# Two ConvLSTM recurrences: seven packed 128-row operands in place of nine 112-row ones, and whole-row elementwise operations

## The reference, cut to what matters

```python
def _convlstm_scan(x_rows, w_mid, b, reverse):
    # x_rows: (H, B, C, W); w_mid: (4*HC, C+HC, 3)
    def step(carry, xr):
        h, c = carry
        inp = jnp.concatenate([xr, h], axis=1)
        gates = lax.conv_general_dilated(inp, w_mid, (1,), 'SAME', dimension_numbers=dn) + b[None, :, None]
        i, f, g, o = jnp.split(gates, 4, axis=1)
        c2 = jax.nn.sigmoid(f) * c + jax.nn.sigmoid(i) * jnp.tanh(g)
        h2 = jax.nn.sigmoid(o) * jnp.tanh(c2)
        return ((h2, c2), h2)
    _, hs = lax.scan(step, (z, z), x_rows, reverse=reverse)
    return hs
```

## Time and profile before

| | |
|---|---|
| Time, median of 3 runs (lowest to highest) | 2120.07 us (2117.99 to 2121.75) |
| The profiled execution: time, span of its instructions | 2124.06 us, 2122.2 us |
| PE matmul busy | 1832.6 us (86%) |
| DVE busy | 1387.2 us (65%) |
| ACT busy | 1066.5 us (50%) |
| POOL busy | 765.1 us (36%) |
| Mean granted TensorE clock | 0.936 |
| DMA | 111.26 MB, 20.7% of the 16 engines' span |

### The profile page before, as it was taken

How to read it: one execution, slowest core, us unless ns; L and a number is a source line. 1 busy time by engine, 2 the same in 40 slices (tenths; PEclk the granted TensorE clock), 3 DMA queues, 4 the chain that set the end, 5 groups by cost and what they waited for, 6 DMA issues and landing times. The chain is left out here.

```text
span 2122.2 us, 43782 instructions
## 1 busy us (share of the span) xinstructions
PE 1832.6 (86%) x16306; PEld 1197.3 (56%) x16306; DVE 1387.2 (65%) x2552; ACT 1066.5 (50%) x1961; POOL 765.1 (36%) x581
## 2 busy tenths in 40 slices
PE   6979179999999998459999999998503999999999
PEld 5535157777777775137777777776101455555555
DVE  5539968888888886658888888888541333333334
ACT  1116147777777775737777777776611222222220
POOL 2010055666666653036666566564029000000000
PEclk9989689999999999769999999999756999999999
DMA  2769420000000000930000000000760011101100
GB/s 74 250 193 201 105 54 22 22 24 22 22 24 22 22 24 13 168 97 23 24 22 23 23 22 24 22 22 9 125 170 0 3 32 32 33 18 33 32 18 25
DMA packets 74138, 111.26 MB, mean 52 GB/s; under 512 B 11248, under 2 KB 30560, under 8 KB 74032
## 3 DMA queue, kind: packets, MB, share of 16 engines
q1 hardware_dynamic: 74032, 109.65, 20.7%
HBM read 71.87 MB, written 37.75 MB: 52 GB/s over the span
## 5 line engine op out<-in xcount | busy, mean ns | idle before, releaser
L668 PE MATMUL gates_l<-xh_l,w_hi_l 112*112 112x512 f32 x3072 | 819.7, 402 | 106.3 <-DVE keep_l L730 106.3
L668 PEld LDWEIGHTS gates_l<-xh_l,w_hi_l 112*112 112x112 f32 x3072 | 537.9, 175 | 304.8 <-issue 107.2
L644 POOL TENSOR_TENSOR xh_l<-xf_l,xh_l 48x512 fp32r<-48x512 f32 x256 | 359.9, 1406 | 281.8 <-ACT xh_l L687 281.3
L668 PE MATMUL gates_l<-xh_l,w_lo_l 112*112 112x512 f32 x1536 | 450.4, 402 | 0.0
L639 POOL TENSOR_TENSOR xh_l<-hs,xh_l 48x512 fp32r<-48x512 f32 x254 | 303.6, 1195 | 173.7 <-DVE hs L759 173.7
L668 PEld LDWEIGHTS gates_l<-xh_l,w_lo_l 112*112 112x112 f32 x1536 | 270.0, 176 | 98.0
L1132 PE MATMUL b_dw<-b_hid,b_diag 32*32 32x512 f32 x9120 | 312.4, 599 | 0.0
L699 ACT ACTIVATE gate_if_l<-gates_l 112x512 f32<-112x512 f32 x256 | 153.4, 599 | 246.0 <-PE gates_l L668 246.0
L739 DVE TENSOR_TENSOR keep_l<-gate_if_l,cell_l 48x512 f32<-48x512 f32 x256 | 175.5, 686 | 140.7 <-ACT gate_if_l L699 140.7
L1132 PEld LDWEIGHTS b_dw<-b_hid,b_diag 32*32 32x32 f32 x9120 | 186.4, 103 | 114.4 <-issue 46.9
L748 DVE TENSOR_TENSOR cell_l<-keep_l,add_l 48x256 f32<-48x256 f32 x512 | 196.8, 428 | 26.6
(11 more groups left out here) (148 smaller groups left out, 1288.3 us busy)
## 6 DMA issues: line engine op xcount, KB each, us to landing
xf_l<-rows SPq DMA_DIRECT2D x256, 96.0 KB, 2.0
hs<-rows SPq DMA_DIRECT2D x32, 384.0 KB, 10.6
rows<-hs SPq DMA_DIRECT2D x32, 384.0 KB, 5.1
xr<-in_x_rows SPq DMA_DIRECT2D x24, 256.0 KB, 2.7
xc<-in_x_cols SPq DMA_DIRECT2D x24, 256.0 KB, 3.0
mixed<-stage SPq DMA_DIRECT2D x24, 256.0 KB, 3.0
edged<-stage SPq DMA_DIRECT2D x24, 256.0 KB, 3.2
mixed_sb<-mixed SPq DMA_DIRECT2D x32, 192.0 KB, 7.3
```

Of the source, the lines that this page charges most:

```text
L644: pool.tensor_tensor(xh[far[d]:far[d] + C, d, s, 1, :, 1:W + 1], xf[far[d]:far[d] + C, s, :].rearrange("p (b w) -> p b w", b=B), xh[far[d] ...
L668: mm = nc.tensor.matmul(ps[d][m][0:K, :], weight[:, d, m, t, :], xh[0:K, d, s, part, :, t:t + W], start=(first and t == 0), stop=(last and ...
```

## The change

The nine operands of 112 rows become seven of 128 rows. The 16 rows beside each 48 (48 to 63 and 112 to 127), which were padding, now hold 32 of the 48 x channels in their high part. The other 16 channels of x, with their three taps laid side by side on the partitions, once for the high and once for the low part of the weights, and the bias, make one operand of their own (xc). So the operands are: xc once; three taps of the tile HI (high part of h, low part of x, 32 channels of the high part of x); three taps of the tile LO (low part of h, a copy of the high part of h, the same 32 channels). With two halves m of the gates there are 14 matmuls in a half-step.

To fill these rows, ACT rounds both directions' x of a row in one operation of 112 rows into a new tile xs (split_hi, L746), copies the high part of the state to the far partitions (copy_state, L752), and SP copies the 16-row pieces within SBUF by four DMAs for each half-step (spread, L628 and L633). The low part of x (split_lo) now waits until the matmuls of two rows before have read the tile.

The elementwise work loses its halves: one tanh of the cell over 512 columns, one product for h_hi. tanh(g) is written in place in PSUM, i*g too, and the cell and its tanh take one bank of PSUM each for both directions. Before the loop, the weights (1568 KB in place of 588 KB) are loaded into the unused part of hs, rounded with two casts and turned into low parts by four masked operations. ACT begins its first split_hi only when DVE has set the first values of the semaphores behind these.

The diff, cut to its core:

```diff
+                def spread(d, s):
+
+                    for a in range(2):
+                        some = x_rows(s, slice(far[d] + a * GAP, far[d] + (a + 1) * GAP)).bitcast(F32)
+                        sp.dma_start(xh[a * HALF + C:(a + 1) * HALF, d, s, :, :].bitcast(F32), some.unsqueeze(1).broadcast_to([GAP, 2, FLAT])
+                                     ).then_inc(x_spread[d][s], 16)
+                    rest = xs[far[d] + 2 * GAP:far[d] + C, s, LEAD - 1:LEAD - 1 + FLAT].bitcast(F32)
+                    shifts = bass.AP(rest.tensor, rest.offset, [list(rest.ap[0]), [1, 3], [1, FLAT]])
+                    for c in range(2):
+                        sp.dma_start(xc[3 * GAP * c:3 * GAP * (c + 1), d, s, :].bitcast(F32), shifts).then_inc(x_spread[d][s], 16)
...
+                    sp.wait_ge(x_hi, s + 1)
+                    for d in range(2):
+                        spread(d, s)
+                sp.wait_ge(x_lo[0], 1)
+                sp.wait_ge(x_lo[1], 1)
+                load(2, H - 3, 0)
...
+                        done, ahead, split = (held(sp, 2 * k + (s + n)) for n in (1, 2, 3))
+                        row_f, row_b = split, held(sp, k * -2 + (H - 4 - s))
+                        if s < more:
+
+                            sp.wait_ge(x_lo[0], ahead)
+                            sp.wait_ge(x_lo[1], ahead)
+                            load(row_f, row_b, 1 - s)
+                        for d in range(2):
+                            sp.wait_ge(gates[d][1], done)
+                            if d == 0:
+                                sp.wait_ge(x_hi, split)
+                            spread(d, s)
...
+                            pe.wait_ge(x_spread[d][s], SPREAD * k + SPREAD)
+                            pe.wait_ge(sig_if[d], 2 * k + (s + 1))
+                            pe.wait_ge(sig_o[d], 2 * k + (s + 1))
+                            pe.wait_ge(cells[d], 2 * k + (s + 1))
+                            for m in range(2):
+                                chunk(m, 0, xc[:, d, s, :], 1, first=True)
+                            pe.wait_ge(x_lo[d], 2 * k + (s + 1))
+                            pe.wait_ge(h_hi[d], 2 * k + (s + 1))
...
+                                    chunk(m, 1 + t, xh[:, d, s, HI, :], t)
+                            pe.wait_ge(h_copy[d], 2 * k + (s + 1))
+                            pe.wait_ge(h_lo[d], 2 * k + (s + 1))
...
+                                for t in range(3):
+                                    mm = chunk(m, 4 + t, xh[:, d, s, LO, :], t, last=(t == 2))
+                                mm.then_inc(gates[d][m], 1)
...
+                    act.wait_ge(h_hi[d], 1)
+                    act.wait_ge(cells[d], 1)
+
+                def split_hi(t, r):
+
+                    act.wait_ge(x_in[r], 16 * t - 16 * r + 32)
+                    if not (isinstance(t, int) and t < 2):
+
+                        for d in range(2):
+                            act.wait_ge(x_spread[d][r], (t - r) * (SPREAD // 2))
+                            act.wait_ge(x_lo[d], t - 1)
+                    nc.scalar.activation(inner(x_rows(r, slice(0, K))), wide(xf[0:K, r, :]), ACT.Copy).then_inc(x_hi, 1)
+
+                def copy_state(t, d, s):
+
+                    n, f = near[d], far[d]
+                    act.wait_ge(h_hi[d], t + 1)
+                    nc.scalar.activation(inner(xh[f:f + C, d, s, LO, :]), inner(xh[n:n + C, d, s, HI, :]).bitcast(F32),
+                                         ACT.Copy).then_inc(h_copy[d], 1)
+                for r in range(3):
+                    split_hi(r, r % 2)
+                copy_state(0, 0, 0)
...
+                            if d == 0:
+                                copy_state(2 * k + s, 1, s)
+                            elif not (last and s == 1):
+                                copy_state(2 * k + (s + 1), 0, 1 - s)
+                            act.wait_ge(cells[d], 2 * k + (s + 2))
+                            nc.scalar.activation(tanh_c[f:f + C, :], cell[f:f + C, :], ACT.Tanh).then_inc(tanhs[d], 1)
+                        if s < more:
+                            split_hi(2 * k + (s + 3), 1 - s)
...
+                dve.wait_ge(w_loaded, 32)
+                per_d = NCH * 2 * K
+                for d in range(2):
+                    nc.vector.tensor_copy(w[:, d].rearrange("p a b c -> p (a b c)"), raw[:, d * per_d:(d + 1) * per_d]
+                                          ).then_inc(w_hi, 1)
+                for d in range(2):
+                    dve.wait_ge(w_hi, d + 1)
+                    for q, chunks in enumerate((slice(0, 1), slice(1, 4))):
+                        part = w[:, d, chunks].rearrange("p a b c -> p (a b c)")
+                        whole = raw[:, d * per_d + chunks.start * 2 * K:d * per_d + chunks.stop * 2 * K]
+                        nc.vector.scalar_tensor_tensor(part, part.bitcast(F32), mask[:, d, q:q + 1], whole, ALU.mult, ALU.add
+                                                       ).then_inc(w_ready, 1)
+                dve.wait_ge(cleared, 3)
+                for d in range(2):
+                    for i, first in enumerate((h_hi[d], h_lo[d], sig_if[d], sig_o[d])):
+                        nc.vector.memset(begun[:, 4 * d + i:4 * d + i + 1], 0.0).then_inc(first, 1)
...
+                            nc.vector.tensor_tensor(ps[d][1][n:n + C, :], gate_if[n:n + C, d, :], ps[d][1][n:n + C, :],
...
+                            nc.vector.tensor_tensor(cell[f:f + C, :], keep[n:n + C, :], ps[d][1][n:n + C, :], ALU.add
+                                                    ).then_inc(cells[d], 1)
+                            dve.wait_ge(sig_o[d], 2 * k + (s + 2))
+                            dve.wait_ge(tanhs[d], 2 * k + (s + 1))
+                            nc.vector.tensor_tensor(inner(xh[n:n + C, d, 1 - s, HI, :]), wide(gate_o[f:f + C, d, :]),
+                                                    wide(tanh_c[f:f + C, :]), ALU.mult).then_inc(h_hi[d], 1)
```

More of the change, by code:

```diff
@@ L539, in lstm_scans @@
     K = HALF + C
-    PART = HB * W
-    parts = [slice(j * PART, (j + 1) * PART) for j in range(2)]
+    GAP = HALF - C
+    FLAT = B * WP
+    LEAD = 2
     with ctx:
@@ L650, in _, with step @@
                         split_lo(s, d, s)
-                step(0)
-                with pool.Fori(1, H // 2 - 1) as k:
+                def step(k, last=False):
+                    for s in range(2):
+                        for d in range(2):
+                            if not last:
+                                split_lo(2 * k + (s + 2), d, s)
+                            if not last or s == 0:
+                                state_lo(2 * k + s, 2 * k + s if d == 0 else k * -2 + (H - 1 - s), d, s)
+                with pool.Fori(0, H // 2 - 1) as k:
                     step(k)
@@ L661, in _, with chunk @@
                         for d in range(2):
-                            pe.wait_ge(x_lo[d], 2 * k + s + 1)
-                            pe.wait_ge(h_hi[d], 2 * k + s + 1)
-                            def taps(m, weight, part, first, last):
+                            def chunk(m, q, tile, lo, first=False, last=False):
+                                return nc.tensor.matmul(ps[d][m][0:K, :], w[:, d, q, m, :], padded(tile)[:, :, lo:lo + W],
+                                                        start=first, stop=last)
@@ L667, in taps @@
+                            for m in range(2):
                                 for t in range(3):
-                                    mm = nc.tensor.matmul(ps[d][m][0:K, :], weight[:, d, m, t, :],
-                                                          xh[0:K, d, s, part, :, t:t + W],
-                                                          start=(first and t == 0), stop=(last and t == 2))
-                                return mm
+                                    chunk(m, 1 + t, xh[:, d, s, HI, :], t)
@@ L703, in step @@
-                            if not last:
-                                split_hi(k + 1, d, s)
-                            for j, part in enumerate(parts):
-                                act.wait_ge(cells[d], 4 * k + 2 * s + (j + 3))
-                                nc.scalar.activation(tanh_c[f:f + C, j, 0:PART], cell[f:f + C, j, 0:PART],
-                                                     ACT.Tanh).then_inc(tanhs[d], 1)
-                with act.Fori(0, H // 2 - 1) as k:
-                    step(k)
```

235 lines of the change are left out of this document (113 added, 122 removed).

## The result

| | before | after |
|---|---|---|
| Time, median of 5 runs (lowest to highest) | 2121.35 us (2117.99 to 2124.64) | 2137.75 us (2136.33 to 2145.22) |
| Ratio, after to before (95% interval) | | 1.0086 (1.0064 to 1.0108) |
| Profiled execution: time, span | 2124.06, 2122.2 | 2141.19, 2139.4 |
| First DMA of the first layer to its first sigmoid | 16.7 us | 32.1 us |
| Mean half-step | 4.293 us | 4.231 us |

The changed kernel is slower by 0.9%: 16.4 us by the medians, 17.2 us by the spans. Of the 17.2, the two starts add 15.4 and 15.3, together 30.7, the 254 half-step intervals give back 254 x 0.062 = 15.8, and the two tails add 2.4. What is left is -0.1. Three of the 23 executions of the kernel before that experiments 1 to 4 are compared with took 2211 to 2221 us, a slower state that occurs now and then, and the ratios leave them out.

The account below looks back on a forecast made before the run. DVE's cycle through the tanh was taken to bound the half-step at 4.24 us, saving 14 us, with later starts adding 28: 2124.06 - 14 + 28 = 2138, less 4.0 for the median, 2134 us; range 2100 to 2172.

Parts of the forecast that it names:

- DVE's cycle: From one h_hi to the next, through all DVE operations of a half-step and one tanh: 4.24 us against 4.295.
- The upper bounds: DVE's cycle with every term at its upper bound, given as 4.35 us.
- PE's 3.34: 14 matmuls at 0.239 us per half-step; rival that PE stays the bound, 1906 us, chance 0.02.
- the lower ones: DVE's cycle with every term at its lower bound, given as 4.03 us.
- hs to keep, held: On DVE, the other direction's keep is held until hs ends: 0.68 and 0.03, a step of 0.71 us.
- The rival cycle of 4.14: On DVE, hs and the next keep overlap, giving 4.14 us; part of the shorter-cycle rival, chance 0.22.
- tanh to h_hi, 0.10 because of two waits: Hand-over from ACT's tanh to L823 takes 0.10 us, not 0.03, since L823 has two waits.
- from add to cell: On DVE, 0.10 us from the end of add to cell, which needs add's result.
- The start: Each layer's first DMA to its first sigmoid takes 31 us; 14 us later per layer, 28 in all.
- SP: Ten DMA issues a row take 4.5 us of 8.48; rival that SP or DMAs bound, 2210 us, chance 0.04.
- Who releases PE before LO: Sign in the profile: PE idle before a half-step's first LO matmul, put down to POOL's h_lo.
- The tail: The end of each layer stays as it was.

Follow-up runs that it names:

- Experiment 1: Changed kernel with the two waits ahead of state product L823 swapped, the tanh wait now written first: 2121.49 us, 16.3 us faster than the changed kernel.
- experiment 2: Changed kernel with each layer's start reordered (x split before DVE's first values, first state copied earlier, row 2 loaded between copies): 2119.35 us.
- Experiment 3: Changed kernel with cell sum, tanh and state product again in two halves, a PSUM bank for each half of cell and tanh: 2037.03 us.
- experiment 4: Kernel before, nine operands, with cell sum, its tanh and state product as one whole-row operation each: 2424.05 us, ratio 1.1417.
- 6: Changed kernel with each xc matmul issued twice, 16 matmuls a half-step in place of 14: 2139.40 us, ratio 1.0089.
- 5: Kernel before with whole-row cell sum, tanh and state product, and tanh(g) and i*g in place in PSUM: 2122.72 us, ratio 1.0009.
- 8: Changed kernel with tanh(g) and i*g in SBUF tiles in place of PSUM: 2470.65 us, ratio 1.1655.

## Why the prediction was right, point by point

- **DVE's cycle.** Forecast 4.24 us, measured 4.231. Its terms were met to 0.02: add's step 0.81 for 0.79, tanh and its hand-over 0.66 for 0.68, the tanh itself 0.562 for 0.58. The gain was 15.8 us for 14. Experiments 1 and 6 show that this cycle is the bound and PE is not; 3 shows that the stall beside the tanh is what keeps the seven operands from paying. The upper bounds add up to 4.34, not 4.35, and PE's 3.34 is a sixth under the sum of the lower ones, not a fifth; neither changes anything.
- **hs to keep, held.** hs ends at 602.17 and keep starts at 602.20, 0.03 behind. The rival cycle of 4.14 rested on an overlap there, and no row shows one.
- **tanh to h_hi, 0.10 because of two waits.** Experiment 1 forecast 17.5 us for this and measured 16.3. The prediction gave another reason for the same 0.10 from add to cell, that the cell needs add's result. But L819 has two waits as well, and the late one, on add, is the separate one; in the changed kernel it starts 0.10 behind add. How much of that 0.10 is the order was not tried.
- **The start.** Forecast 31 us, measured 32.1 and 32.0, or 15.4 more in a layer for 14. The chain was right but for its first link, where the memsets and not the weights come last; that the sum came so close is luck, since errors of some 3 us in its terms cancelled. The weights had landed before the memsets ended, so the cast began at 9.4 us. The two casts took 1.86 us for 3.0 to 3.7, and DVE was done at 13.7 for 17. The copies cost 0.67 us each to issue, not 0.45, so that SP was through with copies and loads at 26.8 for 26; the three matmuls and their end took 1.7 for 1.2. The forecast's own steps behind the 26, 2.2 and 1.3, add up to 29.5, not 29.8. The price of the casts came from a row of before that had a hidden partner, POOL's split_lo, in the same stretch:

```profile
275.71 6.63 POOL L644 TENSOR_TENSOR xh_l<-xf_l,xh_l 48x512 fp32r<-48x512 f32 x4 [1.91 <-ACT xh_l L687]
```

- **SP.** In the steady part a copy takes 0.62 to 0.63 us and a load 0.32, so ten issues take 5.6 us of 8.46, not 4.5. There is still room, and no load or copy releases ACT or PE there.
- **Who releases PE before LO.** Forecast POOL's h_lo. From 310 to 830 us PE waited 62 times for POOL's L674 (22.6 us) and 61 times for ACT's copy_state (21.7 us): the two end almost together, in turn. This changed no time, since PE is not the bound.
- **The tail.** Forecast as unchanged, but it is 1.2 us longer in each layer. The last sigmoid now ends early and its keep waits in DVE's queue (837.85 and 839.26, 1.41 us apart, where the earlier trace rows have 0.71 from 600.02 to 600.73), and the stall of the last half-step is part of the tail as well.
- **Size.** 2134 us forecast, 2137.75 measured. The 3.8 us are the starts (2.7), the tails (2.4), less 1.8 from the cycle; the other 0.5 is that the median lies 3.4 and not 4.0 under the profiled execution.

The prediction priced the seven operands and the whole-row operations together. Experiment 3 takes them apart: with the halves kept the changed kernel is 4.0% faster than the one before, later starts included, and the whole rows undo that. It still has tanh(g) and i*g in PSUM. What the seven operands would be worth with both in SBUF was not tried; experiments 4, 5 and 8 show that with whole rows the place alone is worth over 300 us in either kernel.

## What to carry to other kernels

When the busiest engine gets shorter, add up the cycle that runs through the queue of the next one, hand-overs and stalls included, before counting operations: two halves that overlap another engine can be worth more than the fixed cost that one whole operation saves. Take the price of an operation from a row only after looking at what the other engines did in the same stretch. Where an operation has two waits and one is always late, see which of them the compiled program takes first, and make it take the late one last; in this kernel that means to write the late wait first in the code.

## What the runs showed of the hardware that was not expected

**DVE operations with two inputs in SBUF and POOL's operations on SBUF hold each other up.** Experiments 4 and 5 differ in the place of i*g and tanh(g) alone, and so do 8 and the changed kernel: 1236 and 1512 ns against 697, and for POOL's split_lo 1645 against 1192. With one input in PSUM an operation of DVE is not touched: L815, 602.91 to 603.61, starts inside POOL's L674, 602.35 to 603.54, and takes 0.70. The 753 ns of L743 against 686 of L739 in the earlier trace rows were this, seen in the mean: 242 of the 256 L743 overlap L639 and take 756 ns on average, the other 14 take 687. The Trainium skill has it as a rule ("SBUF — State Buffer", section "SBUF: two separate sides"): the two engines share one pair of ports, and whichever starts first keeps it for its whole instruction. The ends in experiment 4 agree with that, 0.55, 1.05 and 0.56 us after the other's. The rule takes in some one-input operations too; the two casts of experiment 2, 3.39 us beside POOL and 1.86 without, agree. POOL's timeline of the kernel before, beside the earlier trace rows, shows the same two distances:

```profile
600.46 1.20 POOL L639 TENSOR_TENSOR xh_l<-hs,xh_l 48x512 fp32r<-48x512 f32 x1 [0.68 <-DVE hs L759]
602.68 1.45 POOL L644 TENSOR_TENSOR xh_l<-xf_l,xh_l 48x512 fp32r<-48x512 f32 x1 [1.02 <-ACT xh_l L687]
```

Add ends at 602.21, 0.55 after L639, and L644 ends at 604.13, 1.05 after the second half of the cell (603.08).

**The order of two waits on one instruction counts.** With the late one taken first L823 started 0.10 us after the tanh, in all 256 half-steps, and with it last 0.03. The wait on its own and the operation behind it lie 0.07 apart in the trace; why they do stays open.

That experiment 4 lost 303 us, while the kernel before, with the same tiles in SBUF but in halves, loses next to nothing, has to do with when the operations meet. Before, add starts 0.22 us before L639 ends and loses 0.07, and the cell is already under way when L644 starts, so that it is POOL that waits; all of it is hidden behind PE's 4.29 us. In experiment 4 add starts 0.65 before L639 ends, and L644 starts 0.69 before the cell. Whether the halves or the moment alone make this was not tried.
